# Routed experts of a decoder layer on one core: 17 tiles of 256 slots and 6 of 128 in place of 23 of 256

## The chip, the core and the metric

The kernel runs on one core of a Trainium2 chip. The metric is the device time in microseconds, the median of some runs. A core has TensorE (matmuls; PE in the profile, and PEld for its weight loads), VectorE (DVE), ScalarE (ACT), GpSimd (POOL) and SyncE (SP), which issues most transfers. Each engine works through its own instructions in order, and they wait for each other on semaphores.

## The reference

One decoder layer on x of shape (4, 512, 512): a gated linear recurrence, cross attention over 1601 context rows, and a block of causal self attention and a mixture of experts. Each is added to x, and a layer norm follows. The change lies in the experts:

```python
h = _rms(x, w_ln2).reshape(B * S, H)            # 2048 rows of 512
probs = jax.nn.softmax(h @ w_router, axis=-1)   # 8 experts
top_w, top_i = jax.lax.top_k(probs, TOP_K)      # 2 for each row
g = jnp.einsum('th,ehi->eti', h, w_gate_e)      # inner width 352
u = jnp.einsum('th,ehi->eti', h, w_up_e)
y = jnp.einsum('eti,eih->eth', jax.nn.silu(g) * u, w_down_e)
routed = jnp.einsum('eth,te->th', y, combine)   # combine: top_w at top_i, else 0
sh = jax.nn.silu(h @ w_sh_gate) * (h @ w_sh_up) @ w_sh_down    # inner width 1408
sh = sh * jax.nn.sigmoid(h @ w_sh_eg)
x = x + (routed + sh).reshape(B, S, H)
```

## The kernel before

The last stage, `moe`, runs through a list of passes (`schedule`). Passes 0 to 11 are the shared expert on batches 0 and 1, in six units of its inner width. Then there are 23 routed tiles, one pass each. Then come 12 passes of the shared expert on batches 2 and 3. A pass computes gate and up products, chunk by chunk of the inner width (128, 128 and 96 for a routed tile), with the weights stationary and the rows of the tile moving. Every f32 product is done as three fp32r matmuls, hi x hi, lo x hi and hi x lo (`product3`), over four chunks of 128 inputs. So a routed chunk has 12 matmuls for gate and 12 for up, and a tile has 72, each with its own weights to load.

Each row of the input goes to two experts. So 4096 (row, expert) pairs are sorted by expert into slots. A tile of `TW` = 256 slots belongs to one expert. An expert's last tile is filled up with whatever lies in the slots. The count of rows of each expert is known on the chip only, so the number of tiles is the one that always suffices: 4088 // 256 + 8 = 23. Which expert's weights a tile takes is computed by VectorE in `places`: it counts tiles for each expert (`few`, `many`), sums them up (`upto_e`), moves each row's place behind the tiles of the experts before (`place`), and compares the running sums with each tile's number (`compared`, `expert`). GpSimd then scatters the rows into `slots` in DRAM (32 indirect transfers), and for each tile it picks the expert's weights by indirect transfers: `pick_up` twice (gate and up, 0.72 MB each, into the single buffer `up_raw`) and `pick_down` (0.79 MB, into `dn_raw`). A pick is issued when the weights before it in that buffer have been split into hi and lo.

Around a tile x, in TensorE's order: chunk 0 of x (24 matmuls); the down product of tile x - 1 (`down`: for each block of 128 rows 9 matmuls of 512 columns, with the activations stationary); gate of chunk 1; the transposes of the rows of tile x + 1 (`turn`: 8 of 128 x 128); up of chunk 1; chunk 2. `down` of a tile waits until VectorE has written the low part of its last activations (`low_act(2)`).

ScalarE's order in a pass: sigmoid(0), split_up of the next tile's gate weights, high_act(0), split_up of its up weights, the copies of the previous tile's y out of PSUM (one for each block of 128 rows), sigmoid(1), high_rows of the next tile (4), split_down, high_act(1), sigmoid(2), high_act(2). VectorE follows with gated(0), split_up, low_act(0), split_up, low_rows (4), gated(1), split_down, low_act(1), gated(2), low_act(2). gated is two multiplications: by the sigmoid, and by the up product. SyncE loads the rows of tile x + 2 after the transposes of x + 1, and stores y block by block. The slots of y are gathered and added to X during the second shared part (`combine`).

`places` runs on VectorE at the end of pass 0.

Of the kernel before, what the change touches and what calls it, by code (L numbers as in the profile page):

```python
# [16 lines left out]
ALU = mybir.AluOpType  # L17
ACT = mybir.ActivationFunctionType
AX_X = mybir.AxisListType.X

P = 128
# [1902 lines left out]
TW = 256  # L1924
NTILES = (B * T * 2 - NEXP) // TW + NEXP
SLOTS = NTILES * TW

# [31 lines left out]
def moe(nc, X, regions, ahead, hx, slots, ident, d, out):  # L1959
# [21 lines left out]
    with ExitStack() as stack:  # L1981
# [18 lines left out]
        before = m.sb("before", [P, NEXP, NEXP])  # L2000
        above = act_f.bitcast(BF16).rearrange("p (t i j) -> p t i j", t=NTILE, i=NEXP)
        equal_f = S.tile("m_equal", at_s, NTILE * NEXP * NEXP // 2)
        equal = equal_f.bitcast(BF16).rearrange("p (t i j) -> p t i j", t=NTILE, i=NEXP)
        compared = equal_f[:, 0:NTILES * NEXP].rearrange("p (j e) -> p j e", e=NEXP)
# [16 lines left out]
        many = m.sb("many", [P, NEXP])  # L2021
        upto_e = m.sb("upto_e", [P, NEXP])
        picked = m.sb("picked", [P, NTILE, NEXP])
        expert = m.sb("expert", [P, NTILES])
        slot = m.sb("slot", [P, 2, NTILE], mybir.dt.int32)
        up_row = m.sb("up_row", [P, 2, NTILES], mybir.dt.int32)
# [30 lines left out]
        def _(sp):  # L2057
# [26 lines left out]
            def store_rows(tile):  # L2084
                for s in range(TW // P):
                    n = tile * (TW // P) + s
                    sp.wait_ge(s_ye, n + 1)
                    sp.dma_start(yslots[n * P:(n + 1) * P], ys[:, n % NY]).then_inc(s_ys[n % NY], 16)
# [31 lines left out]
        def _(pool):  # L2120
# [5 lines left out]
            pool.iota(count_i[:], pattern=[[1, NTILES]], base=0, channel_multiplier=0).then_inc(s_const, 1)  # L2126
            pool.iota(part_i[:], pattern=[[0, 1]], base=0, channel_multiplier=1).then_inc(s_const, 1)
            pool.wait_ge(s_const, 7)
# [21 lines left out]
            def pick_up(tile):  # L2150
                for j in range(2):
                    pool.wait_ge(s_uplo[j], UNITS + tile)
                    pool.indirect_dma_start(up_raw[:, j].rearrange("p k n -> p (k n)"), None, d["up"],
                                            bass.IndirectOffsetOnAxis(up_row[:, j, tile:tile + 1], 0)).then_inc(s_up_picked[j], 16)

            def pick_down(tile):
                pool.wait_ge(s_dnlo, UNITS + tile)
                if tile == 0:
                    for i in range(RINGS):
                        pool.wait_ge(s_scat[i], 16 * 2 * len(range(i, NTILE, RINGS)))  # L2160
                pool.indirect_dma_start(dn_raw[:].rearrange("p i n -> p (i n)"), None, d["dn"],
                                        bass.IndirectOffsetOnAxis(dn_row[:, tile:tile + 1], 0)).then_inc(s_dn_picked, 16)
# [8 lines left out]
            for i in range(NY):  # L2171
                pool.wait_ge(s_ys[i], 16 * len(range(i, NTILES * TW // P, NY)))
# [13 lines left out]
        def _(act):  # L2186
# [18 lines left out]
            def high_rows(tile):  # L2205
                if tile >= 2:
                    act.wait_ge(s_gu, 2 * base(R0 + tile - 1))
                if tile == 0:
                    act.wait_ge(s_gu, 2 * base(R0 - 1))
                if tile == 1:  # L2210
                    act.wait_ge(s_gu, 2 * base(R0))
                for k in range(KC):
                    act.wait_ge(s_tt, 2 * tile + k // 2 + 1)
                    act.activation(t_hi[tile % 2][:, k, :], t_bank[k // 2][:, (k % 2) * TW:(k % 2 + 1) * TW], ACT.Copy,
                                   scale=w2[:, k:k + 1]).then_inc(s_thi, 1)
# [7 lines left out]
            for x in passes:  # L2223
                p, w = x.p, x.stage
                width = T if x.shared else TW
# [49 lines left out]
        def _(dve):  # L2275
# [11 lines left out]
            def gated(x, i):  # L2287
                n, rows, width = base(x.p) + i, x.chunks[i][1], T if x.shared else TW
# [9 lines left out]
            def low_act(x, i):  # L2298
                n, rows, width = base(x.p) + i, x.chunks[i][1], T if x.shared else TW
# [18 lines left out]
            dve.wait_ge(s_const, 10)  # L2318
# [13 lines left out]
            own.done(dve.tensor_copy(part_f[:], part_i[:]))  # L2332

# [6 lines left out]
            few = equal_f[:, 0:NEXP * NEXP].rearrange("p (e k) -> p e k", e=NEXP)  # L2340
            start = count_f[:, 0:NEXP].unsqueeze(1).to_broadcast([P, NEXP, NEXP])
            own.done(dve.scalar_tensor_tensor(few, start, float(TW), total.unsqueeze(2).to_broadcast([P, NEXP, NEXP]), ALU.mult, ALU.is_lt))
# [10 lines left out]
            def places():  # L2353
                own.done(dve.tensor_reduce(many[:], few, AX_X, ALU.add))
                own.wait()
                own.done(dve.tensor_tensor_scan(upto_e[:], ones[:, 0:NEXP], many[:], 0.0, ALU.mult, ALU.add))
                own.wait()
                own.done(dve.tensor_tensor(many[:], upto_e[:], many[:], ALU.subtract))
                own.wait()
                own.done(dve.scalar_tensor_tensor(by_expert(place[:]), many[:].unsqueeze(2).to_broadcast([P, NEXP, NTILE]), float(TW), by_expert(place[:]), ALU.mult, ALU.add))  # L2360
                own.done(dve.tensor_tensor(compared, upto_e[:].unsqueeze(1).to_broadcast([P, NTILES, NEXP]),
                                           count_f[:].unsqueeze(2).to_broadcast([P, NTILES, NEXP]), ALU.is_le))
# [34 lines left out]
            def low_rows(tile):  # L2397
                for k in range(KC):
                    dve.wait_ge(s_thi, KC * tile + k // 2 * 2 + 2)
                    dve.scalar_tensor_tensor(t_lo[tile % 2][:, k, :], t_bank[k // 2][:, (k % 2) * TW:(k % 2 + 1) * TW], w2[:, k:k + 1],  # L2400
                                             t_hi[tile % 2][:, k, :], ALU.mult, ALU.subtract).then_inc(s_tlo, 1)
# [71 lines left out]
        def _(pe):  # L2473
            def turn(tile):
# [5 lines left out]
                for k in range(KC):  # L2480
                    for s in range(TW // P):
# [26 lines left out]
            for x in passes:  # L2508
                p, w = x.p, x.stage
                if x.shared:  # L2510
                    hi, lo, width = h_hi[x.group], h_lo[x.group], T
                else:
                    hi, lo, width = t_hi[x.tile % 2], t_lo[x.tile % 2], TW
# [4 lines left out]
                for i, (r0, rows) in enumerate(x.chunks):  # L2518
# [3 lines left out]
                    for j in range(2):  # L2522
                        if n == 0:
                            pe.wait_ge(s_uplo[j], 1)
                        if i == 1 and j == 1 and p + 1 < NP and not passes[p + 1].shared:
                            turn(passes[p + 1].tile)
                        product3(pe, gu_bank[n % 2][j][0:rows, 0:width],
                                 lambda c: up_hi[:, w % 2, j, c, r0:r0 + rows], lambda c: up_lo[:, w % 2, j, c, r0:r0 + rows],
                                 lambda c: hi[:, c, :], lambda c: lo[:, c, :], KC).then_inc(s_gu, 1)
                    if i == 0 and p:  # L2530
                        down(passes[p - 1])
                    if i == 1:
                        if p == 0:
                            pe.wait_ge(s_mask, 1)
                            pe.wait_ge(s_const, 10)
# [99 lines left out]
```

## Time and profile before

| | |
|---|---|
| median of 3 runs | 2493.06 us (2492.18 to 2497.55) |
| profiled execution, its own time | 2495.78 us |
| its span, first to last instruction | 2494.1 us |
| TensorE busy | 2374.0 us, 95% |
| weight loads | 1537.8 us, 62% |
| VectorE, ScalarE, GpSimd busy | 1353.1, 1351.2, 927.6 us |
| mean granted TensorE clock | 0.99 of full speed |

The span and the time of one execution differ by what lies before the first and after the last instruction. Matmul records overlap, since a matmul is recorded until its last result is out. So the rate of TensorE is read from the distances between starts and not from the mean durations. Weight loads overlap each other in the same way.

### The profile page before, as it was taken

Reading aid. Unit: us, or ns where it says so; the run is one execution under the profiler, and the core shown is the slowest. Engines: PE = TensorE matmul, PEld = TensorE weight load, DVE = VectorE, ACT = ScalarE, POOL = GpSimd, SP = SyncE. Lnnn points to the kernel's source line nnn. Section 1 sums busy time; section 2 is a strip of 40 time slices with the busy share of each in tenths; the row PEclk is TensorE's granted clock in tenths of the full one; section 3 lists DMA queues with packets and bytes.
Section 4 is the critical chain, followed back from the end, with each engine's and each line's share of the span. In section 5 each row is a group of like instructions: output and inputs, shape, how many; then the busy total and the mean of one; then the engine's idle time right before and its main releaser. Section 6 shows DMA issues by size and latency. Waiting matters only on the chain. (4 is left out here: it accounts for less than half of the span.)

```text
span 2494.1 us, 39149 instructions
## 1 busy us (share of the span) xinstructions
PE 2374.0 (95%) x15376; PEld 1537.8 (62%) x15376; DVE 1353.1 (54%) x2105; ACT 1351.2 (54%) x1714; POOL 927.6 (37%) x610
## 2 busy tenths in 40 slices
PE   8999899999999999999998899998899999999997
PEld 6877444444444444444334556565588899999885
DVE  6676534434443434443413755555565677776785
ACT  4332577677766777667995443433422366665221
POOL 1237654565465535654212433332033021221320
PEclk9999899999999999999999999999899999999999
DMA  6003774667455764756745000001144277775430
GB/s 219 17 18 106 221 197 117 157 167 194 118 146 158 196 170 97 186 155 167 191 87 203 18 1 18 1 18 54 60 163 160 92 238 243 243 237 185 144 119 34
DMA packets 206935, 331.46 MB, mean 133 GB/s; under 512 B 71264, under 2 KB 125792, under 8 KB 206560
## 3 DMA queue, kind: packets, MB, share of 16 engines
q1 hardware_dynamic: 188256, 252.80, 35.8%
q0 software_dynamic: 16336, 72.23, 8.8%
q10 hardware_dynamic: 2160, 3.93, 0.5%
q8 instruction: 122, 2.00, 0.3%
q14 instruction: 61, 0.50, 0.1%
HBM read 241.53 MB, written 99.42 MB: 137 GB/s over the span
## 5 line engine op out<-in xcount | busy, mean ns | idle before, releaser
L1052 ACT ACTIVATE A_c_prob<-c_psum 128x1024 f32<-128x1024 f32 x832 | 786.8, 1029 | 277.4 <-PE c_psum L1302 271.3
L982 POOL TENSOR_TENSOR E_c_roots<-E_c_roots,c_half 128x32 f32<-128x32 f32 (+1 forms) x70 | 363.3, 5191 | 406.6 <-DVE E_c_roots L1069 406.5
L1311 PE MATMUL c_psum<-A_c_prob,c_vq 128*17 128x512 f32 x3328 | 415.4, 599 | 8.6 <-DVE c_oT L1204 8.3
L137 PE MATMUL c_psum<-E_c_w,E_c_c 128*128 128x512 f32 x1248 | 313.8, 401 | 3.1 <-DVEq L1189 2.2
L1302 PE MATMUL c_psum<-c_qq,c_kq 64*128 64x512 f32 x1664 | 287.9, 438 | 18.8 <-ACT A_c_prob L1052 11.3
L137 PEld LDWEIGHTS c_psum<-E_c_w,E_c_c 128*128 128x128 f32 x1248 | 227.4, 188 | 124.6 <-issue 41.0
L1302 PEld LDWEIGHTS c_psum<-c_qq,c_kq 64*128 64x128 f32 x1664 | 136.6, 185 | 167.2 <-ACT A_c_prob L1052 91.4
L1108 DVE COPY E_c_unit<-c_psum 128x256 f32<-128x256 f32 x89 | 37.8, 425 | 327.8 <-PE c_psum L137 327.8
L2504 PE MATMUL m_psum<-A_m_dn_hi,A_m_a 128*128 128x512 f32 (+1 forms) x628 | 204.3, 394 | 2.2 <-DVE A_m_a L2301 2.2
L137 PE MATMUL m_psum<-R_m_t,m_up_hi 128*128 128x256 f32 (+1 forms) x1104 | 200.0, 283 | 0.0
L1311 PEld LDWEIGHTS c_psum<-A_c_prob,c_vq 128*17 128x17 f32 x3328 | 68.6, 96 | 188.4 <-issue 163.7
L1742 DVE TENSOR_REDUCE s_topx<-s_psum 128x4 f32<-128x2048 f32 (+1 forms) x64 | 95.5, 1492 | 146.2 <-PE s_psum L1860 137.0
L137 PEld LDWEIGHTS m_psum<-R_m_t,m_up_hi 128*128 128x128 f32 (+1 forms) x1104 | 165.8, 179 | 2.1
L2240 ACT ACTIVATE A_m_a<-Q_m_work 128x256 fp32r<-128x256 f32 (+2 forms) x113 | 56.7, 502 | 200.9 <-DVE Q_m_work L2296 159.2
L137 PE MATMUL m_psum<-R_m_t,m_up_lo 128*128 128x256 f32 (+1 forms) x552 | 154.7, 280 | 0.0
L1653 ACT ACTIVATE A_s_pT<-s_psum 128x2048 f32<-128x2048 f32 (+1 forms) x64 | 79.5, 1242 | 121.2 <-PE s_psum L1874 120.9
L2504 PEld LDWEIGHTS m_psum<-A_m_dn_hi,A_m_a 128*128 128x128 f32 (+1 forms) x628 | 117.8, 188 | 28.6 <-DVE A_m_a L2301 2.7
L137 PE MATMUL r_psum<-E_x,E_w_hi 128*128 128x512 f32 x384 | 121.0, 397 | 10.0 <-DVE E_w_lo L414 9.2
L2233 ACT ACTIVATE Q_m_work<-m_psum 128x256 f32<-128x256 f32 (+2 forms) x113 | 51.9, 459 | 134.2 <-PE m_psum L137 134.2
L2504 PE MATMUL m_psum<-Q_m_dn_lo,A_m_a 128*128 128x512 f32 (+1 forms) x314 | 123.1, 392 | 0.0
L975 POOL TENSOR_TENSOR E_c_c<-E_c_raw,E_c_c 128x512 fp32r<-128x512 f32 x89 | 118.7, 1333 | 7.1
L137 PE MATMUL m_psum<-R_g_hi,m_up_hi 128*128 128x512 f32 x264 | 105.6, 400 | 3.6 <-DVE m_up_lo L2278 3.6
(316 smaller groups left out, 4216.7 us busy)
## 6 DMA issues: line engine op xcount, KB each, us to landing
c_kq<-kd SPq DMA_DIRECT2D x248, 208.0 KB, 6.1
kd<-S_c_t SPq DMA_DIRECT2D x96, 256.0 KB, 4.0
E_c_raw<-in_ctxT SPq DMA_DIRECT2D x89, 256.0 KB, 4.2
qd<-A_c_q SPq DMA_DIRECT2D x64, 256.0 KB
c_qq<-qd SPq DMA_DIRECT2D x64, 256.0 KB, 3.1
vd<-A_c_vt SPq DMA_DIRECT2D x104, 136.0 KB, 3.0
c_vq<-vd SPq DMA_DIRECT2D x31, 442.0 KB, 9.0
R_m_hs<-slots SPq DMA_DIRECT2D x23, 512.0 KB
```

What stands on the lines that cost most here:

```text
L137: mm = pe.matmul(out, a(c), b(c), start=first and i == 0, stop=last and i == len(terms) - 1)
L975: pool.tensor_tensor(c_lo[:, job % 2], c_raw[:, n % CB], c_hi[:, job % 2], ALU.subtract).then_inc(s_clo, 1)
L982: pool.tensor_tensor(rr[:, unit % RB, 0:n], ms[:, unit % RB, 0:n], half[:, 0:n], ALU.pow).then_inc(s_r, 1)
L1052: act.activation(prob[:, t % PB, 2 * (u % 2):2 * (u % 2) + 2, :], score_banks[u % 3], ACT.Exp, scale=XD ** -0.5).then_inc(s_ex, 1)
L1108: dve.tensor_copy(raw[:, unit % RB, at:at + HD], src[:, 0:HD]).then_inc(s_k, 1)
L1302: mm = pe.matmul(score_banks[u % 3][:, s, :], kq[rows, q % 2, u % 2, kt * P:(kt + 1) * P], qq[rows, q % 2, u % 2, :], start=True, stop=True)
L1311: mm = pe.matmul(o_bank[32 * j:32 * j + VW, :], vq[:, q % 2, kt, j, :], prob[:, t % PB, j, :], start=kt == 0, stop=kt == CT - 1)
L1653: act.activation(pT[:, kt % 2, :, 0:L], psum[:, 0:HPC, 0:L], ACT.Exp, scale=SCALE).then_inc(s_ex, 1)
L1742: dve.reduce_max(topx[:, t, ::SD], psum[:, 0:HPC, 0:(t + 1) * P], AX_X).then_inc(s_top, 1)
L2233: act.activation(sig[0:rows, 0:width], gu_bank[n % 2][0][0:rows, 0:width], ACT.Sigmoid).then_inc(s_sig, 1)
L2240: act.activation(a_hi[0:rows, p % 2, i, 0:width], act_f[0:rows, 0:width], ACT.Copy).then_inc(s_ahi, 1)
L2504: mm = pe.matmul(y_bank[t], a[0:rows, p % 2, i, ts], w[0:rows, i, :], start=k == 0, stop=k == 3 * len(x.chunks) - 1)
```

## The change

There are still 23 tiles, but 17 of them are pairs of halves (256 slots) and 6 are single halves (128 slots), 40 halves in all against 46. An expert with n rows gets full pairs for its rows; if the number of its halves is odd, the last half goes to a single, and when the singles are used up, to a pair of its own where room is. The tiles are worked on in the order pair, pair, pair, single, five times over, and then pair, pair, single. All widths of a routed pass follow `x.width`, 256 or 128. `places` computes the new positions and the experts of the tiles.

```diff
-NTILES = (B * T * 2 - NEXP) // TW + NEXP
-SLOTS = NTILES * TW
+PAIRS, SINGLES = 17, 6
+HALVES = 2 * PAIRS + SINGLES
+NTILES = PAIRS + SINGLES
+SLOTS = HALVES * P
+def order_of_tiles():
+    out, pair = [], 0
+    for single in range(SINGLES):
+        upto = min(3 * single + 3, PAIRS)
+        out += [*range(pair, upto), PAIRS + single]
+        pair = upto
+    return out
+ORDER = order_of_tiles()
+first_half = lambda column: 2 * column if column < PAIRS else column + PAIRS
...
-        self.subs = TT if self.shared else TW // P
+        self.subs = TT if self.shared else 1 + (ORDER[tile] < PAIRS)
+        self.width = self.subs * P
...
-                rows = slots[tile * TW:(tile + 1) * TW].rearrange("(s p) n -> p s n", p=P)
-                sp.dma_start(hs[:, tile % 2], rows).then_inc(s_hs[tile % 2], 16)
+                at, subs = first_half(ORDER[tile]), passes[R0 + tile].subs
+                rows = slots[at * P:(at + subs) * P].rearrange("(s p) n -> p s n", p=P)
+                sp.dma_start(hs[:, tile % 2, 0:subs], rows).then_inc(s_hs[tile % 2], 16)
...
-            pool.iota(count_i[:], pattern=[[1, NTILES]], base=0, channel_multiplier=0).then_inc(s_const, 1)
+            pool.iota(count_i[:, 0:PAIRS], pattern=[[2, PAIRS]], base=0, channel_multiplier=0).then_inc(s_const, 1)
+            pool.iota(count_i[:, PAIRS:NTILES], pattern=[[1, SINGLES]], base=2 * PAIRS, channel_multiplier=0).then_inc(s_const, 1)
+            pool.iota(ranks_i, pattern=[[1, 2 * NEXP]], base=0, channel_multiplier=0).then_inc(s_const, 1)
...
-                                            bass.IndirectOffsetOnAxis(up_row[:, j, tile:tile + 1], 0)).then_inc(s_up_picked[j], 16)
+                                            bass.IndirectOffsetOnAxis(up_row[:, j, ORDER[tile]:ORDER[tile] + 1], 0)).then_inc(s_up_picked[j], 16)
...
             def places():
-                own.done(dve.tensor_reduce(many[:], few, AX_X, ALU.add))
+                own.done(dve.tensor_scalar(below, ranks_f[:, 0:NEXP], -float(NEXP), None, ALU.add))
+                own.done(dve.tensor_reduce(np_e, few[:, :, 1::2], AX_X, ALU.add))
+                own.done(dve.tensor_reduce(ns_e, few[:, :, 0::2], AX_X, ALU.add))
...
+                own.done(dve.scalar_tensor_tensor(turn_e, singles_e, pairs, ns_e, ALU.add, ALU.subtract))
+                own.wait()
+                own.done(dve.tensor_scalar(single_at, turn_e, float(PAIRS), pairs, ALU.min, ALU.max))
+                own.wait()
+                own.done(dve.tensor_tensor(single_at, single_at, turn_e, ALU.add))
...
-                    for s in range(TW // P):
+                    for s in range(passes[R0 + tile].subs):
...
-                        product3(pe, gu_bank[n % 2][j][0:rows, 0:width],
+                        product3(pe, gu_bank[n % 2][j][0:rows, 0:x.width],
                                  lambda c: up_hi[:, w % 2, j, c, r0:r0 + rows], lambda c: up_lo[:, w % 2, j, c, r0:r0 + rows],
-                                 lambda c: hi[:, c, :], lambda c: lo[:, c, :], KC).then_inc(s_gu, 1)
+                                 lambda c: hi[:, c, 0:x.width], lambda c: lo[:, c, 0:x.width], KC).then_inc(s_gu, 1)
```

In `places`, 20 VectorE instructions stand in place of 5; the part shown as "..." goes on in the manner of the lines around it. `high_rows`, `low_rows`, `gated`, `low_act`, `sigmoid` and `high_act` take `width` where they had 256.

## Rows read from the trace of the kernel before

**Rows 1.** The page, busy time of the engines.
```profile
PE 2374.0 (95%) x15376; PEld 1537.8 (62%) x15376; DVE 1353.1 (54%) x2105; ACT 1351.2 (54%) x1714; POOL 927.6 (37%) x610
```

**Rows 2.** Chain that ended last, in order of time: start, us, what.
```profile
1795.32 13.95 PE m_psum L137 x48
...
1831.62 5.48 PE m_psum L2504 x24
...
2095.31 0.88 PE m_psum L2482 x8
2096.18 7.10 PE m_psum L137 x60
2103.29 4.25 PE m_psum L2504 x18
2107.54 1.43 PE m_psum L137 x12
```

**Rows 3.** Timeline, the transposes in a routed pass: start, us, engine, line, operation.
```profile
2108.70 0.90 PEld L2482 LDWEIGHTS m_psum<-ident,R_m_hs 128*128 128x128 f32 x8
```

**Rows 4.** Timeline of TensorE in the first stage.
```profile
54.61 0.95 PE L551 MATMUL r_psum<-r_ones,r_sumsq 128*128 128x1 f32 x8
...
55.42 0.48 PE L137 MATMUL r_psum<-E_w_hi,E_o 128*128 128x512 f32 x1
```

**Rows 5.** Timeline of TensorE, attention scores with 128 moving columns.
```profile
1495.51 0.40 PE L1868 MATMUL s_psum<-Q_s_qk,Q_s_qk 32*128 32x128 f32 x8
...
1495.73 0.28 PE L1872 MATMUL s_psum<-s_negm,s_sel 32*128 32x128 f32 x4
```

**Rows 6.** Groups by line and shape, weight loads: busy us, mean ns.
```profile
L137 PEld LDWEIGHTS m_psum<-R_m_t,m_up_hi 128*128 128x128 f32 x736 | 114.6, 188 | 2.1
L137 PEld LDWEIGHTS m_psum<-R_m_t,m_up_hi 128*96 128x96 f32 x368 | 51.2, 162 | 0.0
```

**Rows 7.** Timelines of TensorE, ScalarE, VectorE and GpSimd in one routed pass.
```profile
2123.23 0.48 PE L137 MATMUL m_psum<-R_m_t,m_up_hi 128*128 128x256 f32 x2
...
2130.42 0.46 PE L2504 MATMUL m_psum<-A_m_dn_hi,A_m_a 128*128 128x512 f32 x1
...
2124.58 1.50 ACT L2203 ACTIVATE A_m_dn_hi<-Q_m_dn_raw 128x1536 fp32r<-128x1536 f32 x1
...
2131.66 1.37 ACT L2194 ACTIVATE m_up_hi<-S_up_raw 128x1408 fp32r<-128x1408 f32 x1
...
2124.01 1.66 DVE L2400 SCALAR_TENSOR_TENSOR R_m_t<-m_psum,S_w,R_m_t 128x256 fp32r<-128x256 f32 x4 [2.65 <-ACT R_m_t L2214]
...
2129.91 0.42 DVE L2301 TENSOR_TENSOR A_m_a<-Q_m_work,A_m_a 96x256 fp32r<-96x256 f32 x1 [0.48 <-ACT A_m_a L2240]
...
2121.63 0.94 POOL L2153 DMA_INDIRECT S_up_raw<-in_up,m_up_row  x1 [0.99 <-DVE m_up_lo L2278]
```

**Rows 8.** Two stretches: busy us of each engine, granted clock, DMA share, GB/s.
```profile
2128.30:2129.10 0.80, 0.80 (x9) 0.80 (x8) 0.68 (x3) 0.00 (x0) 0.70 (x1) 1.00 0.09 37
2133.10:2133.90 0.80, 0.80 (x5) 0.67 (x4) 0.80 (x2) 0.41 (x1) 0.55 (x1) 1.00 0.00 0
```

**Rows 9.** Timeline of VectorE in passes 0 and 1.
```profile
1809.88 0.29 DVE L2338 TENSOR_TENSOR S_m_place<-S_m_place,m_psum 128x128 f32<-128x128 f32 x1
...
1814.59 0.21 DVE L2354 TENSOR_REDUCE m_many<-S_m_equal 128x8 f32<-128x64 f32 x1
...
1815.45 0.34 DVE L2361 TENSOR_TENSOR S_m_equal<-m_upto_e,m_count_f 128x184 f32<-128x184 f32 x1
...
1818.96 0.69 DVE L2293 TENSOR_TENSOR Q_m_work<-m_psum,Q_m_work 128x512 f32<-128x512 f32 x1
...
1827.55 0.69 DVE L2301 TENSOR_TENSOR A_m_a<-Q_m_work,A_m_a 128x512 fp32r<-128x512 f32 x1 [0.70 <-ACT A_m_a L2240]
```

**Rows 10.** What touches the slots: count, ns least/median/most, first and last start.
```profile
L2082 SPq DMA_DIRECT2D R_m_hs<-slots x23: 360/439/649, 1959.0 to 2258.7; - x23
...
L2147 POOL DMA_INDIRECT slots<-A_m_spare,m_slot x16: 959/972/1922, 1825.6 to 1914.3; - x16
```

More of the change, by code:

```diff
@@ L2020, in moe @@
         rank = S.tile("m_rank", at_s + NEXP * NTILE, NTILE, NEXP)
-        many = m.sb("many", [P, NEXP])
-        upto_e = m.sb("upto_e", [P, NEXP])
+        np_e, ns_e, pairs_e, singles_e, pair_at, turn_e, single_at, shift, below = (restart[:, i * NEXP:(i + 1) * NEXP] for i in range(9))
         picked = m.sb("picked", [P, NTILE, NEXP])
@@ L2211, in high_rows @@
                     act.wait_ge(s_gu, 2 * base(R0))
+                width = passes[R0 + tile].width
                 for k in range(KC):
                     act.wait_ge(s_tt, 2 * tile + k // 2 + 1)
-                    act.activation(t_hi[tile % 2][:, k, :], t_bank[k // 2][:, (k % 2) * TW:(k % 2 + 1) * TW], ACT.Copy,
+                    act.activation(t_hi[tile % 2][:, k, 0:width], t_bank[k // 2][:, (k % 2) * TW:(k % 2) * TW + width], ACT.Copy,
                                    scale=w2[:, k:k + 1]).then_inc(s_thi, 1)
@@ L2224, in _ @@
                 p, w = x.p, x.stage
-                width = T if x.shared else TW
+                width = x.width
                 prev = passes[p - 1] if p else None
@@ L2287, in gated @@
             def gated(x, i):
-                n, rows, width = base(x.p) + i, x.chunks[i][1], T if x.shared else TW
+                n, rows, width = base(x.p) + i, x.chunks[i][1], x.width
                 dve.wait_ge(s_sig, n + 1)
@@ L2298, in low_act @@
             def low_act(x, i):
-                n, rows, width = base(x.p) + i, x.chunks[i][1], T if x.shared else TW
+                n, rows, width = base(x.p) + i, x.chunks[i][1], x.width
                 dve.wait_ge(s_ahi, n + 1)
@@ L2332, in _ @@
             own.done(dve.tensor_copy(part_f[:], part_i[:]))
+            own.done(dve.tensor_copy(ranks_f[:], ranks_i))
             by_expert = lambda ap: ap.rearrange("p (e t) -> p e t", e=NEXP)
@@ L2339, in _ @@
             total = by_expert(upto[:])[:, :, NTILE - 1]
-            few = equal_f[:, 0:NEXP * NEXP].rearrange("p (e k) -> p e k", e=NEXP)
-            start = count_f[:, 0:NEXP].unsqueeze(1).to_broadcast([P, NEXP, NEXP])
-            own.done(dve.scalar_tensor_tensor(few, start, float(TW), total.unsqueeze(2).to_broadcast([P, NEXP, NEXP]), ALU.mult, ALU.is_lt))
+            few = few_f.rearrange("p (e k) -> p e k", e=NEXP)
+            start = ranks_f[:].unsqueeze(1).to_broadcast([P, NEXP, 2 * NEXP])
+            own.done(dve.scalar_tensor_tensor(few, start, float(P), total.unsqueeze(2).to_broadcast([P, NEXP, 2 * NEXP]), ALU.mult, ALU.is_lt))
             own.wait()
@@ new lines, in places @@
+                own.done(dve.scalar_tensor_tensor(turn_e, singles_e, pairs, ns_e, ALU.add, ALU.subtract))
[3 more added lines that the diff above has]
+                own.done(dve.tensor_tensor(single_at, single_at, turn_e, ALU.add))
+                own.wait()
+                own.done(dve.scalar_tensor_tensor(shift, pairs_e, -2.0, single_at, ALU.mult, ALU.add))
+                own.done(dve.scalar_tensor_tensor(by_expert(behind), each(np_e), float(TW), placed, ALU.mult, ALU.is_le))
@@ new lines, in places @@
+                own.done(dve.tensor_tensor(ns_e, ns_e, below, ALU.mult))
+                own.wait()
+                own.done(dve.tensor_tensor(by_expert(behind), by_expert(behind), each(shift), ALU.mult))
+                own.done(dve.scalar_tensor_tensor(placed, each(pair_at), float(TW), placed, ALU.mult, ALU.add))
+                own.done(dve.scalar_tensor_tensor(compared, per_tile(pairs_e), 2.0, halves, ALU.mult, ALU.is_le))
+                own.done(dve.tensor_tensor(matched, per_tile(single_at), halves, ALU.is_equal))
@@ L2363, in places @@
+                own.wait()
+                own.done(dve.scalar_tensor_tensor(place[:], behind, float(P), place[:], ALU.mult, ALU.add))
+                own.done(dve.tensor_tensor(matched, matched, per_tile(ns_e), ALU.mult))
+                own.wait()
+                own.done(dve.tensor_tensor(compared, compared, matched, ALU.add))
                 own.wait()
@@ L2480, in turn @@
                 for k in range(KC):
-                    for s in range(TW // P):
+                    for s in range(passes[R0 + tile].subs):
                         tr = pe.transpose(t_bank[k // 2][:, (k % 2) * TW + s * P:(k % 2) * TW + (s + 1) * P],
@@ L2510, in _ @@
                 if x.shared:
-                    hi, lo, width = h_hi[x.group], h_lo[x.group], T
+                    hi, lo = h_hi[x.group], h_lo[x.group]
                 else:
-                    hi, lo, width = t_hi[x.tile % 2], t_lo[x.tile % 2], TW
+                    hi, lo = t_hi[x.tile % 2], t_lo[x.tile % 2]
                     pe.wait_ge(s_tlo, KC * (x.tile + 1))
```

39 lines of the change are left out of this document (24 added, 15 removed).

## The prediction

> **What bounds the kernel now.** The page comes first: TensorE is busy for 95% of the span, VectorE and ScalarE for 54% each [rows 1], and the mean granted clock is 0.99, its upper level nearly throughout. The chain that ended last is to be read next. From 1795 us on, through the expert stage up to the last pass, it consists of TensorE alone [rows 2]. A routed tile repeats four pieces: 8 transposes in 0.87 us, 60 product matmuls in 7.10, 18 down matmuls in 4.25, 12 product matmuls in 1.43. Their sum is 13.65 us, and 23 tiles have this period. So whatever shortens TensorE's stream in a tile counts in full, until another engine or a transfer becomes late. The rates in that stream: 7.10/60 = 118.3 ns a product matmul of 256 columns, 4.25/18 = 0.236 us a down matmul of 512 columns, 0.87/8 = 0.109 us a transpose.
>
> **The change, step by step.** The number of tiles stays 23, so the weight picks (46 and 23 indirect transfers), the weight splits and the 72 product matmuls a tile stay. Six tiles have 128 slots instead of 256. In such a tile:
> - One block of 128 rows instead of two goes through the down product: 9 matmuls fewer, 9 x 0.236 = 2.12 us.
> - 4 transposes fewer: 4 x 0.109 = 0.44 us.
> - 72 product matmuls stream 128 columns instead of 256. Each still loads its own weights, and here is the choice on which the sum hangs. If only columns counted, a matmul would fall to about 60 ns: from 512 to 256 columns it falls by 118 ns, 0.46 a column, and 118.3 - 128 x 0.46 = 59. But three places show a floor above that. Transposes with 128x128 weights and 128 moving columns start every (0.90 - 0.14)/7 = 0.109 us [rows 3]. In the first stage, eight matmul records with 128x128 weights and a single moving column begin at 54.61 and the next matmul at 55.42: 0.81/8 = 0.101 us, though there is hardly anything to stream [rows 4]. And in the attention scores, whose operands are fp32r tiles as here and whose moving side has 128 columns, eight matmuls (two sets of four that run side by side, 32 rows each) take from 1495.51 to the next set at 1495.73, 0.11 us a set [rows 5]. All of this fits one load of 128 weight columns. The load records agree: 188 ns for 128 columns, 162 for 96 [rows 6], that is 0.81 ns a column on a fixed part, so about 104 ns of loading proper for 128 columns. I take 0.109 us for the 48 matmuls of the two 128-row chunks. They save 48 x 0.0093 = 0.45 us.
> - The third chunk has 96 weight columns. No row shows it with few moving columns. From the records it loads 26 ns faster, 0.083 us, and 24 matmuls save 24 x 0.035 = 0.85 us. The other bound is 0.108 us, if what rows 5 show is the moving side at half rate and not the load: then 24 x 0.010 = 0.24 us. I take 0.083, because with one moving column the floor is nearly as high [rows 4], which a moving side can't cause.
>
> Sum for a small tile: 2.12 + 0.44 + 0.45 + 0.85 = 3.86 us; six give 23.2 us (19.5 with the other value for the 96 columns).
>
> The Trainium skill (TensorE: Matmul & The Clock Gate, section LDWEIGHTS) puts a load at columns/1.2 ns, which is 107 and 80 ns, and says that row count does not matter. By its figures the sum would be 48 x 0.012 + 24 x 0.038 + 2.56 = 4.05 us a tile, 24 in all; it speaks for the 0.083, and for carrying rows 5, with 32 rows, over to 128.
>
> **What could become late.** The saving is spread over three passes, since a pass holds the down product of the tile before it and the transposes of the one behind it. The pass before a small tile takes 13.65 - 0.44 = 13.2 us, its own 13.65 - 1.30 = 12.35, the one after it 13.65 - 2.12 = 11.5. No pass falls to the 9.8 that a small tile alone would make.
>
> The nearest wait today is that of the down product for the low part of the last chunk (low_act): VectorE starts it at 2129.91 and needs 0.42, and the down product starts at 2130.42, so 0.1 us is left [rows 7]. Walk the same chain behind a small tile. The transposes in its pass end at T (2123.23 in the rows' pass; the down product starts at T + 7.2 there). ScalarE's high_rows and split_down keep their size, and VectorE's split_down can start where ScalarE's ends, at T + 2.9 (2126.08). It takes 1.7 to the next start, low_act(1) 0.36, gated(2) 0.6, ScalarE 0.33, low_act(2) 0.3: T + 6.2. The short ones are scaled to what 128 x 128 elements cost in rows, 0.29 us [rows 9]. TensorE arrives at T + 12 x 0.109 + 24 x 0.083 + 24 x 0.118 and the 0.1 which the rows' pass has on top: T + 6.2. So this is even, and costs 0 to 0.1 us a tile. Ahead of a small tile its first chunk takes 2.6 us instead of 2.84, but its narrow high_rows and low_rows release the engines 0.4 us earlier: 0.35 us left.
>
> Behind a small tile VectorE also loses 2.12 us between its last split_up and low_rows (2124.01), where it now idles for 2.65 [rows 7]: 0.5 us stays.
>
> The picks: both up transfers are issued by 2122.6, and the engines' DMA share is near 1 until 2128.3, then 0.09 for 0.8 us [rows 7, 8]; ScalarE takes up the second half at 2131.66. In a pass of 11.5 us it would do so at 2129.5, 1.2 us after the landing. The down pick, issued behind VectorE's split_down, has landed when the share is 0 (2133.10) and is taken up at 2124.58 + 13.65 = 2138.2, or 2136.1 then. Both are covered. If they were not, each us of lateness would hold ScalarE's queue (the copies of y, sigmoid(1), high_rows) and through them TensorE.
>
> **Routing arithmetic.** `places` gets 20 VectorE instructions for 5. 12 small ones at about 0.2 us, 4 on 128 elements at 0.29, 4 on 184 at 0.34: about 4.9 us, for 1.20 removed (1814.59 to 1815.79) [rows 9]. The 3.7 us delay gated(2) from 1818.96 to 1822.7; its chunk's bank is wanted at 1826.05. low_act of the next chunk ends at 1828.24 now; with idle time of VectorE taken up it would end at 1831.0, wanted at 1831.62 [rows 2, 9]. Covered by some 0.6 us; without cover it would cost up to 3.7 us once. The slots come 3.9 us later, and so do the 32 scatters (the last at 1914.3), while the first load of rows is at 1959.0 [rows 10]: 40 us of cover. Three more iotas and casts of 0.15 us lie in idle time. SP loads and stores less (half of 6 tiles), and waits nowhere new.
>
> **The sum** is made against the profiled execution, 2495.78 us (span 2494.1 and 1.7 around it): 2495.8 - 23.2 = 2472.6, and with 0.3 us for the even wait 2472.9. It ran 2.7 us over the median of the runs, so the forecast for the median is 2470.2, call it 2470.
>
> **Rivals.**
> - A: narrow matmuls run below the load floor. For it: weight loads overlap each other here already (records of 188 ns every 118). Against it: rows 3 to 5. At 60 ns a small tile would save 72 x 0.058 + 2.56 = 6.7 us, but VectorE's chain holds two downs back: the tile's own first chunk lasts 1.4 us against a chain end at 2.3, 0.9 us, and behind the tile 36 x 0.06 + 2.84 + 0.1 = 5.1 stands against 6.2, 1.1 us. So 4.7 us a tile, 28 in all: 2465. The same page of the Trainium skill (section Back-to-back issue gap) has about 81 ns for a sustained pair of load and matmul at 128 columns; by it a tile would save 72 x 0.037 + 2.56 = 5.2 less some 0.9 of waiting, 26 in all, 2467. The trace has no such row for fp32r. 10%.
> - B: the weights arrive too late. Three weight transfers must pass a tile whatever its width. For it: each pick waits for a split, and its buffer is the only one. Against it: some 2.4 us of every 13.65 have a share under 0.1 (three slices of 0.8, two of them among the rows) [rows 8], so 11.2 us would do, and the shortest pass is 11.5. If it held half of the saving back: 2481; all of it: 2493. 11%.
> - C, on the other side: an fp32r matmul with few moving columns is done in two passes, each with its load, as the plain f32 matmuls of rows 4 are (four calls, eight records). Then 0.216 us a matmul, 72 x 0.098 = +7.0 - 2.56 = +4.5 us a tile: 2520. It decides from 0.154 us a matmul on (2.56/72 above 118.3). Against it: rows 5, where fp32r with 128 columns keeps 0.108 us, though with 32 rows only. 5%.
> - D: the 96-column chunk does not gain (moving side at half rate): 2474. It lies inside the forecast's own range.
>
> **Chances and range.** The forecast with D: 74%, its own range 2467 to 2476. A 10%, B 11% (a quarter of it within 0.2% of no change), C and the like 5%. 0.2%, 5 us, is about what a measurement of this kernel tells from no change. Faster 0.92, same 0.03, slower 0.05. To leave no more than two in ten outside, the range goes from 2462, A's less the 2 to 3 us that its waits are uncertain by, to 2479, where B holds back 9 us.
>
> **What would show it.** In the profile after: the product matmuls of the six tiles 0.109 us apart, 0.083 in the third chunk; passes of 13.2, 12.35 and 11.5 us; 9 down matmuls in 2.1 us; no wait of TensorE on VectorE above 0.1 us; the DMA share near 1 for longer. The forecast is wrong if small tiles show other spacings, if ScalarE waits for a pick, or if the chain of waits leaves TensorE.

## The result and the profile after

| | before | after |
|---|---|---|
| median of 4 runs each, side by side | 2495.31 us (2492.18 to 2499.41) | 2474.99 us (2472.85 to 2476.81) |
| profiled execution, its span | 2495.78, 2494.1 us | 2476.71, 2475.0 us |

The ratio is 0.9919, with a 95% interval of 0.9905 to 0.9933: 20.3 us faster. The forecast was 2470.0, in a range of 2462 to 2479. It had taken 23.1 us off a median of 2493.06; with a fourth run the median of before is 2495.31.

The page of the kernel after, busy time (TensorE does 78 matmuls less: 6 x 9 down, 6 x 4 transposes) [rows 1]:

```profile
PE 2357.1 (95%) x15298; PEld 1522.0 (61%) x15298; DVE 1346.1 (54%) x2121; ACT 1341.0 (54%) x1708; POOL 932.0 (38%) x612
```

The chain that ended last, after: start, us, what. It answers to [rows 2]. First a full tile and a small one with its neighbour, then the end of the routed stage:

```profile
2112.05 4.25 PE m_psum L2555 x18
2116.31 1.43 PE m_psum L137 x12
2117.73 0.44 PE m_psum L2533 x4
2118.17 6.91 PE m_psum L137 x60
2125.07 4.22 PE m_psum L2555 x18
2129.29 1.29 PE m_psum L137 x12
2130.59 0.90 PE m_psum L2533 x8
2131.48 6.23 PE m_psum L137 x60
2137.71 2.13 PE m_psum L2555 x9
2139.84 1.43 PE m_psum L137 x12
...
2149.24 4.21 PE m_psum L2555 x18
...
2268.07 10.29 PE m_psum L137 x72
2278.35 2.06 PE m_psum L2555 x9
2280.41 11.14 PE m_psum L137 x48
```

How to read it: the piece of 60 matmuls that begins at 2118.17 holds 36 with 256 columns and the small tile's first 24 with 128. So 24 narrow ones take 6.91 - 36 x 0.1183 = 2.65 us, 0.110 each. The next 12 take 1.29, 0.108 each. The piece at 2131.48 holds 12 more of these (1.30), the 24 of the 96-column chunk, and 24 wide ones (2.84): 6.23 - 1.30 - 2.84 = 2.09 us, 0.087 each. The timeline shows the same directly, every third matmul 0.25 to 0.26 us after the one before:

```profile
2132.61 0.33 PE L137 MATMUL m_psum<-R_m_t,m_up_hi 128*96 128x128 f32 x2
2132.78 0.25 PE L137 MATMUL m_psum<-R_m_t,m_up_lo 128*96 128x128 f32 x1
2132.86 0.33 PE L137 MATMUL m_psum<-R_m_t,m_up_hi 128*96 128x128 f32 x2
```

Per small tile that is 2.12 (4.25 - 2.13, down) + 0.44 (transposes) + 0.19 + 0.14 + 0.87 (the pieces of products: 7.10 - 6.91, 1.43 - 1.29, 7.10 - 6.23) = 3.76 us, six give 22.6. The distances between down products say the same: 13.02, 12.64 and 11.53 us around the small tile instead of three times 13.65, 3.76 in all. Counted as the forecast counts passes, from first product to first product, the same pieces make 13.21, 12.45 and 11.53 (13.65 less 0.44, 1.20 and 2.12), where 13.2, 12.35 and 11.5 were forecast.

Where the time went, for the whole span. From the first routed transposes to the end of the last routed down product, before took 1972.80 to 2300.23, 327.4 us; after took 1975.41 to 2280.41, 305.0 us: 22.4 less. From there to the end of the last down product both take 166.2, from the first product of the stage to the first routed transposes both 177.5. The span is 19.1 shorter. The missing 3.3 us lie outside: 0.7 behind the last down product, and 2.6 ahead of the stage, which begins at 1795.51 instead of 1792.93, in code that the change does not touch. There the granted clock differs. Stretches of after: length, busy us of TensorE, its weight loads, VectorE, ScalarE and GpSimd with their counts, granted clock, DMA share, GB/s:

```profile
1410.00:1420.00 10.00, 8.44 (x82) 4.81 (x80) 5.07 (x7) 3.17 (x3) 3.82 (x3) 0.88 0.00 0
1420.00:1430.00 10.00, 9.31 (x85) 6.29 (x78) 4.74 (x3) 2.95 (x3) 3.62 (x4) 0.60 0.01 2
1740.00:1750.00 10.00, 8.41 (x77) 5.90 (x79) 6.03 (x6) 3.09 (x4) 0.00 (x0) 0.83 0.01 2
```

The same stretches of before are granted 1.00, the whole of the self attention between 1350 and 1760 too. Its score matmuls start over 404.4 us in before (1353.5 to 1757.9) and over 408.2 in after (1352.4 to 1760.6).

### The profile page after: what moved, and what is told of

Its sections match the earlier page's. It is cut to its first block and busy times, and to the rows that moved or that the text cites. A ratio compares the mean times of both kernels' runs of the same rounds, so it can differ in the third digit from the quotient of the medians.

```text
span 2475.0 us, 38993 instructions
## 1 busy us (share of the span) xinstructions
PE 2357.1 (95%) x15298; PEld 1522.0 (61%) x15298; DVE 1346.1 (54%) x2121; ACT 1341.0 (54%) x1708; POOL 932.0 (38%) x612
## 5 line engine op out<-in xcount | busy, mean ns | idle before, releaser
L1302 PE MATMUL c_psum<-c_qq,c_kq 64*128 64x512 f32 x1664 | 288.3, 438 | 19.1 <-ACT A_c_prob L1052 11.2
L2555 PE MATMUL m_psum<-A_m_dn_hi,A_m_a 128*128 128x512 f32 (+1 forms) x592 | 193.9, 396 | 2.2 <-DVE A_m_a L2324 2.2
L137 PE MATMUL m_psum<-R_m_t,m_up_hi 128*128 128x256 f32 (+3 forms) x1104 | 192.8, 278 | 0.0
L2263 ACT ACTIVATE A_m_a<-Q_m_work 128x512 fp32r<-128x512 f32 (+4 forms) x113 | 54.7, 484 | 200.9 <-DVE Q_m_work L2319 199.6
L137 PE MATMUL m_psum<-R_m_t,m_up_lo 128*128 128x256 f32 (+3 forms) x552 | 152.8, 277 | 0.0
L2555 PEld LDWEIGHTS m_psum<-A_m_dn_hi,A_m_a 128*128 128x128 f32 (+1 forms) x592 | 112.0, 189 | 27.4 <-DVE A_m_a L2324 2.9
L2256 ACT ACTIVATE Q_m_work<-m_psum 128x512 f32<-128x512 f32 (+4 forms) x113 | 49.9, 442 | 128.4 <-PE m_psum L137 128.4
L2555 PE MATMUL m_psum<-Q_m_dn_lo,A_m_a 128*128 128x512 f32 (+1 forms) x296 | 116.8, 395 | 0.0
```

Of the source, the lines that this page charges most:

```text
L137: mm = pe.matmul(out, a(c), b(c), start=first and i == 0, stop=last and i == len(terms) - 1)
L1302: mm = pe.matmul(score_banks[u % 3][:, s, :], kq[rows, q % 2, u % 2, kt * P:(kt + 1) * P], qq[rows, q % 2, u % 2, :], start=True, stop=True)
L2256: act.activation(sig[0:rows, 0:width], gu_bank[n % 2][0][0:rows, 0:width], ACT.Sigmoid).then_inc(s_sig, 1)
L2263: act.activation(a_hi[0:rows, p % 2, i, 0:width], act_f[0:rows, 0:width], ACT.Copy).then_inc(s_ahi, 1)
L2555: mm = pe.matmul(y_bank[t], a[0:rows, p % 2, i, ts], w[0:rows, i, :], start=k == 0, stop=k == 3 * len(x.chunks) - 1)
```

## The experiments

Every kernel below is the kernel after with the edit shown. "Routed stage" is the stretch just defined, 327.4 us before and 305.0 after; it does not contain the self attention. The time given is one run beside seven or nine of the kernel before, or a median where an interval stands.

### wide_products: the narrow products streamed wide

```diff
-                        product3(pe, gu_bank[n % 2][j][0:rows, 0:x.width],
+                        product3(pe, gu_bank[n % 2][j][0:rows, 0:T if x.shared else TW],
...
-                                 lambda c: hi[:, c, 0:x.width], lambda c: lo[:, c, 0:x.width], KC).then_inc(s_gu, 1)
+                                 lambda c: hi[:, c, 0:T if x.shared else TW], lambda c: lo[:, c, 0:T if x.shared else TW], KC).then_inc(s_gu, 1)
```

> The changed kernel, but the product matmuls of the six small tiles stream 256 columns again (the upper 128 are results that nobody reads); the down product, transposes, copies and transfers stay small. The routed stage, from the first transposes of routed rows to the end of the last routed tile's down product, took 327.4 us before and 305.0 after. Theory (three separate terms that add up): only 6 x (2.12 + 0.44) = 15.4 us are left of the gain, so 312.1 us. Rival (part of the narrow matmuls' gain is eaten by waits and comes back when they are wide): less than 311.

Measured: 2479.60 us; routed stage 1972.64 to 2283.95, 311.3 us. The expectation had 312.1, or less than 311 for its rival, and the run lies between: 0.8 us below the sum of the separate terms, 0.3 above the bound of the rival. The last routed pieces of its chain:

```profile
2270.65 11.25 PE m_psum L137 x72
2281.90 2.05 PE m_psum L2555 x9
```

Narrowing the products is worth 6.3 us in six tiles, 1.05 a tile, and the rest, 16.1 us or 2.69 a tile, comes from the matmuls that a tile no longer has. The product pieces alone show more (7.13, 1.42 and 7.11 here around the small tile, 6.91, 1.29 and 6.23 in after: 1.23), but the down pieces next to them are shorter here (4.13 and 2.08 against 4.22 and 2.13), which takes 0.14 back. Why they are shorter stays open; it moves the border between the two shares by 0.15 us a tile and leaves their sum.

### cols64: 64 moving columns

The products of a small tile stream 64 columns; the activations of the other half of its rows are made from what lies in PSUM, so what is stored for them is not the reference's.

```diff
-                        product3(pe, gu_bank[n % 2][j][0:rows, 0:x.width],
+                        product3(pe, gu_bank[n % 2][j][0:rows, 0:64 if x.width == P else x.width],
...
-                                 lambda c: hi[:, c, 0:x.width], lambda c: lo[:, c, 0:x.width], KC).then_inc(s_gu, 1)
+                                 lambda c: hi[:, c, 0:64 if x.width == P else x.width], lambda c: lo[:, c, 0:64 if x.width == P else x.width], KC).then_inc(s_gu, 1)
```

> The changed kernel, but the product matmuls of the six small tiles stream only 64 columns: half of a small tile's rows are left out. Theory (a narrow product matmul is bound by the load of its own 128 or 96 weight columns): the spacings stay 0.108 and 0.087 us and the routed stage stays at 305 us, within 0.5. Rival (the moving side runs at half rate when narrow, 0.108 us for 128 columns): the matmuls fall to about half, 3.7 us less a tile, some of it lost again to VectorE's chain; the stage ends at 290 to 297 us.

Measured: 2477.57 us; routed stage 308.0 us. The chain around the same small tile:

```profile
2115.93 6.88 PE m_psum L137 x60
2122.81 4.25 PE m_psum L2555 x18
2127.06 1.26 PE m_psum L137 x12
2128.32 0.92 PE m_psum L2533 x8
2129.25 7.77 PE m_psum L137 x60
2137.01 2.07 PE m_psum L2555 x9
```

Half the moving columns save next to nothing: 6.88 for 6.91, 1.26 for 1.29. So the 0.108 us (128 weight columns) and 0.087 (96) go by the weight columns, and what a matmul streams is hidden. That this is the time of its load is argued from that and from the load records (188 and 162 ns); no run here streams through one load twice. Rival A, which has narrow matmuls run below this floor, is out.

The stage is 3.0 us longer than in after, where 0.5 at most had been expected. It sits in two places, 7.77 instead of 6.23 here and 11.83 instead of 10.29 behind the last small tile. In both the clock fell, in stretches of this kernel that are at 1.00 in after:

```profile
2130.00:2140.00 10.00, 10.00 (x72) 9.63 (x72) 7.97 (x16) 6.46 (x11) 1.59 (x2) 0.83 0.74 273
2270.00:2280.00 10.00, 10.00 (x53) 8.40 (x53) 4.48 (x9) 2.32 (x6) 0.00 (x0) 0.83 0.36 107
```

The timeline shows where, behind the last small tile: the narrow matmuls end with their usual spacing, and the wide ones behind them come 0.43 us apart, and then 0.30 and 0.23 again.

```profile
2271.84 0.48 PE L137 MATMUL m_psum<-R_g_hi,m_up_hi 128*128 128x512 f32 x1
...
2272.51 0.63 PE L137 MATMUL m_psum<-R_g_hi,m_up_lo 128*128 128x512 f32 x1
2272.94 0.63 PE L137 MATMUL m_psum<-R_g_hi,m_up_hi 128*128 128x512 f32 x1
...
2275.07 0.63 PE L137 MATMUL m_psum<-R_g_hi,m_up_lo 128*128 128x512 f32 x1
2275.50 0.46 PE L137 MATMUL m_psum<-R_g_hi,m_up_hi 128*128 128x512 f32 x1
```

0.43 us for 512 columns is the lower of the clock's two levels (1.2 GHz), 0.23 the upper (2.4). It cost 1.54 us at each place, at two of six small tiles, in the one execution of this kernel.

### small_last: six small tiles in a row

```diff
 def order_of_tiles():
-    out, pair = [], 0
-    for single in range(SINGLES):
-        upto = min(3 * single + 3, PAIRS)
-        out += [*range(pair, upto), PAIRS + single]
-        pair = upto
-    return out
+    return list(range(NTILES))
```

> The changed kernel, with the six small tiles one after the other behind the 17 large ones. TensorE's own work is the same, but small passes in a row are 9.9 us long, where the weights' three transfers have to keep up (2.75 MB, 278 GB/s). Theory (transfers are covered: issue to landing of the second up pick shrinks with the rows and the y that are smaller too, to about 5.3 us, and a wait of 0 to 0.2 us a tile on VectorE): 305 to 306 us for the routed stage. Rival (the weights' transfers need 11.2 us a tile): 6 x 1.3 us more, 312 to 314.

Measured: 2476.99 us; routed stage 306.2 us, where 305 to 306 had been expected and 312 to 314 by the rival. (The 2.75 MB of the expectation are the three weight transfers, 2.23, and a small tile's rows and y.) The 4 transposes of the later small tiles begin at 2218.87, 2228.77, 2239.04, 2249.03 and 2259.68: passes of 9.90, 10.27, 9.99 and 10.65 us, against 9.89 for a small tile alone (13.65 - 3.76). First ScalarE's waits for weight transfers from 1990 us on (us in total, times, longest), then two timelines, TensorE's two waits and VectorE ahead of the first of them:

```profile
ACT m_up_hi L2211 <- DMA S_up_raw<-in_up,m_up_row: 2.7, 3, 1.5
```

```profile
2235.55 0.51 PE L2550 MATMUL m_psum<-A_m_dn_hi,A_m_a 128*128 128x512 f32 x1 [0.15 <-DVE A_m_a L2319]
2256.21 0.50 PE L2550 MATMUL m_psum<-A_m_dn_hi,A_m_a 128*128 128x512 f32 x1 [0.27 <-DVE A_m_a L2319]
```

```profile
2234.23 0.29 DVE L2311 TENSOR_TENSOR Q_m_work<-m_psum,Q_m_work 96x128 f32<-96x128 f32 x1 [0.44 <-issue]
```

So even where every pass carries its three transfers, the stage is only 1.2 us longer than in after, and not all of that is theirs. The first wait of TensorE, in the pass of 10.27, comes before ScalarE's first wait for a transfer (one of 0.86 us that ends at 2237.67). Ahead of it VectorE stood still for 0.44 us in front of `gated(2)`, and the profile names no cause. The second, in the pass of 10.65, comes behind ScalarE's longest wait, 1.53 us until 2248.33; this pass is 0.76 us over. Rival B's mechanism exists, but it costs less than 1 us here, and its price begins only below the passes of 11.5 us that the change makes; in after ScalarE waits for no pick.

### p16s7, p16s7_again and after_again: one pair less, one single more

```diff
-PAIRS, SINGLES = 17, 6
+PAIRS, SINGLES = 16, 7
...
-        upto = min(3 * single + 3, PAIRS)
+        upto = (single + 1) * PAIRS // SINGLES
```

> 16 pairs and 7 singles, 39 halves, still 23 tiles, spread evenly. Theory (a tile that is small instead of large is worth 3.76 us wherever it stands): the routed stage 301.2 us, the kernel 3.8 us faster than the changed one. Rival (denser small tiles begin to wait, here two large ones between them at times): 303 us or more.

> The changed kernel unchanged, timed again beside the kernel before and beside p16s7_again. Theory (the routed stage gives 22.4 us and nothing else in the kernel moves; what differs from that in a run is TensorE's clock in code that the change leaves alone): 22 to 23 us faster than before in the median, within 2 of it. Rival (something outside the routed stage costs 2 to 3 us in the changed kernel): 19 to 20 us again.

> 16 pairs and 7 singles again. Theory: 3.5 us faster than after_again (the routed stage took 301.5 us against 305.0). Rival (no seventh gain over the whole kernel): same as after_again within 1 us.

Measured:

| kernel | median us | kernel before beside it | ratio, 95% | routed stage |
|---|---|---|---|---|
| p16s7 | 2469.84 (2468.98 to 2476.92) | 2498.43 | 0.9890, 0.9874 to 0.9907 | 301.6 |
| after_again (kernel after, no edit) | 2474.37 (2471.31 to 2477.72) | 2495.59 | 0.9910, 0.9895 to 0.9924 | 305.1 |
| p16s7_again | 2468.83 (2466.68 to 2472.71) | 2495.59 | 0.9895, 0.9880 to 0.9910 | 301.7 |

The routed stage of p16s7 had been expected at 301.2; its trace is of its slowest run, 2476.92 us, the other three took 2468.98 to 2470.12.

A seventh single costs nothing in room: the most halves that 4096 pairs of row and expert over 8 experts need is 4088 // 128 + 8 = 39, which is 2 x 16 + 7, and 17 and 6 make 40. `places` gives the last half of an expert a free pair first and a single when no pair is free, and it lays a pair beyond the last column of pairs on two singles, so every split of the rows has room.

after_again is 21.2 us faster than the kernel before beside it, between the 22 to 23 expected and the 19 to 20 of the rival, and the interval (19 to 26 us) decides nothing; its routed stage of 305.1 us says that the stage repeats. Side by side the seventh single gains 5.5 us in the medians, more than the 3.5 expected, and the runs of the two overlap (2471.31 to 2477.72, 2466.68 to 2472.71). The traces give 3.4 in the routed stage and 3.6 from the stage's first product to the end of the last routed down product: after_again takes 1796.14 to 2278.77, 482.6 us, and p16s7_again 1791.31 to 2270.37, 479.1. What the medians show beyond that is not the seventh single's: in these two profiled executions the stage starts 4.8 us apart, behind code that is the same. The chain of p16s7_again shows the same pieces for its last small tile as that of after:

```profile
2246.91 6.91 PE m_psum L137 x60
...
2258.03 10.29 PE m_psum L137 x72
2268.32 2.06 PE m_psum L2555 x9
```

### p22s1: one single alone

```diff
-PAIRS, SINGLES = 17, 6
+PAIRS, SINGLES = 22, 1
...
-        upto = min(3 * single + 3, PAIRS)
+        upto = PAIRS
```

> 22 pairs and one single at the end: the new routing arithmetic with hardly any of its use. Theory (a small tile gives 3.7 us wherever it stands, the longer arithmetic of places lies wholly under TensorE's work): routed stage 323.7 us, and from the stage's first product matmul to the first routed transposes 177.5 us as before. Rival (the arithmetic shows): this stretch 178.5 us or more.

Measured: 2492.67 us, one run; routed stage 323.9 us, 3.5 less than before, and the stretch from the first product (1795.51) to the first routed transposes (matmul at 1972.92) 177.4, as in before (1795.32, 1972.64: 177.3). So one single gives one sixth of the saving less 0.2 to 0.3 us, a wait of TensorE on VectorE at 2239.99 that has nothing to do with the single, and the new routing arithmetic, all of which this kernel has, costs TensorE 0.1 us at most.

### places_long: 3.9 us more on VectorE

Ahead of the copy into `slot`, at the end of `places`:

```diff
+                for _ in range(12):
+                    own.done(dve.tensor_tensor(picked[:], rank[:], rank[:], ALU.add))
+                    own.wait()
```

> The changed kernel with 12 more VectorE instructions on 128 x 128 elements at the end of places, each waiting for the one before, 3.8 us in all, whose result is not used. In the changed kernel low_act of the second chunk of pass 1 ends at 1832.7 and TensorE comes to wait for it at 1834.2, so 1.5 us are left. Theory (that is the cover): the down product of pass 1 starts 2.3 us late, the stretch from the first product matmul to the first routed transposes is 179.8 us instead of 177.5, and the routed stage stays 305. Rival (the cover is larger, since VectorE catches up in idle time): 177.5.

Measured: 2478.22 us, one run. TensorE's waits from 1795 to 1980 (the first is there in every kernel, before the stage's first product):

```profile
PE m_psum L137 <- DVE m_up_lo L2301: 3.7, 1, 3.7
PE m_psum L137 <- DVE Q_m_work L2319: 1.4, 1, 1.4
PE m_psum L2558 <- DVE A_m_a L2324: 0.8, 1, 0.8
```

The same moments in its timelines, TensorE's two and VectorE's two:

```profile
1828.43 0.48 PE L137 MATMUL m_psum<-R_g_hi,m_up_hi 128*128 128x512 f32 x1 [1.38 <-DVE Q_m_work L2319]
1835.08 0.50 PE L2558 MATMUL m_psum<-A_m_dn_hi,A_m_a 128*128 128x512 f32 x1 [0.81 <-DVE A_m_a L2324]
```

```profile
1822.75 3.88 DVE L2431 TENSOR_TENSOR m_picked<-S_m_rank 128x128 f32<-128x128 f32 x12
...
1834.33 0.69 DVE L2324 TENSOR_TENSOR A_m_a<-Q_m_work,A_m_a 128x512 fp32r<-128x512 f32 x1 [0.70 <-ACT A_m_a L2263]
```

The stretch from the first product to the first routed transposes is 1796.31 to 1976.37, 180.1 us, against 177.3 in after (179.8 against 177.5 had been expected): of 3.9 us on VectorE 2.75 come through. TensorE first waits for the bank that `gated(2)` empties (1.4), then the down product waits for `low_act` of the next chunk (0.8). The down product starts 38.77 us behind the first product, 36.13 in after, 2.64 late, where 2.3 was expected of it. So the cover that after has left is 1.2 to 1.3 us (3.9 less 2.75 or 2.64). The routed stage is 305.4 us, 0.4 longer: VectorE's stop of 0.44 us in front of `gated(2)` is there once in this kernel too, and the down product behind it starts late, at 1998.09.

## Why the prediction was right, point by point

**The sum of a small tile.** 3.86 us was forecast, 3.76 measured:

| term | forecast | measured |
|---|---|---|
| 9 down matmuls | 2.12 | 2.12 |
| 4 transposes | 0.44 | 0.44 |
| 48 products, 128 weight columns | 0.45 | 0.46 (0.19 + 0.14 + 0.13; 0.110 and 0.108 us each) |
| 24 products, 96 weight columns | 0.85 | 0.74 (0.87 - 0.13; 0.087 us each) |

The mis-sized term is the last: 0.087 us a matmul instead of 0.083, 0.1 us a tile. Cut the other way, by wide_products, the products give 1.05 and the vanished matmuls 2.69; the sum is the same. The choice on which the sum hung, that the weight load is the floor at 128 moving columns [rows 3 to 5], held: cols64 shows that the moving columns are not the floor, and the 96-column chunk that the weight columns are. The load of 96 columns is a shorter one, as the load records of 188 and 162 ns said [rows 6], by 0.021 us for the 0.026 read off them; the other bound, 0.108, is refuted, and rival D with it. The Trainium skill (TensorE: Matmul & The Clock Gate, section LDWEIGHTS) gives by its rule of columns over 1.2 ns an estimate of 107 and 80 ns for these loads; the first agrees with the 0.108 us measured, the second is 0.007 us under the 0.087.

**The narrow matmuls below the floor (A).** Not so: 0.108 to 0.110 with 128 columns, and 0.105 with 64 (1.26 / 12). The same page of the Trainium skill (section Back-to-back issue gap) has about 81 ns for a pair of load and matmul at 128 columns; here, with fp32r operands, it is 108, and the forecast that followed from the 81 ns, 2467, did not come.

**Two passes with a load each (C).** Not so: 0.108 us, where it needed 0.216, with 128 rows as with the 32 of [rows 5].

**The chain behind a small tile.** It was forecast as even. Timelines of VectorE and TensorE, after:

```profile
2137.15 0.29 DVE L2324 TENSOR_TENSOR A_m_a<-Q_m_work,A_m_a 96x128 fp32r<-96x128 f32 x1 [0.38 <-ACT A_m_a L2263]
...
2142.67 1.66 DVE L2451 SCALAR_TENSOR_TENSOR R_m_t<-m_psum,S_w,R_m_t 128x256 fp32r<-128x256 f32 x4 [0.44 <-ACT R_m_t L2237]
```

```profile
2137.55 0.45 PE L2555 MATMUL m_psum<-A_m_dn_hi,A_m_a 128*128 128x512 f32 x1
```

`low_act(2)` ends at 2137.44, the down product starts at 2137.55: 0.1 us left, T + 6.3 with T = 2131.24, where T + 6.2 was forecast. It has no wait beside it, and TensorE waits for nobody in the whole routed stage. So the 0.3 us that the sum had set aside for it were not spent. VectorE's idle time ahead of `low_rows` is 0.44, forecast 0.5.

That 0.1 us is all the cover, and that after never waits is partly luck. In all nine traces of the new code VectorE stands still once in the routed stage, for 0.44 us in front of `gated(2)`, and the profile names no cause. In after it does so in the pass ahead of a small tile, where there is more cover:

```profile
2224.68 0.42 DVE L2316 TENSOR_TENSOR Q_m_work<-m_psum,Q_m_work 96x256 f32<-96x256 f32 x1 [0.44 <-issue]
```

In small_last, p22s1, places_long and both p16s7 kernels it falls elsewhere, and the down product behind it starts 0.3 us late. The prediction has no term for such a stop. It also accounts for most of what the seventh single misses of 3.76 us.

**The picks (B).** Covered, as forecast, at passes down to 11.5 us. GpSimd issues them as before but for the first up pick in the pass of each small tile that still has picks: it is recorded with 2.28 us instead of 0.94 [rows 7], in all five of them, and the second goes out 0.66 us later for it. Why stays open; it held up nothing:

```profile
2127.46 2.28 POOL L2175 DMA_INDIRECT S_up_raw<-in_up,m_up_row  x1 [3.90 <-DVE m_up_lo L2301]
```

small_last ran passes of 9.9 to 10.65 us. So the 11.2 us that the prediction put as the least that the transfers allow was wrong: it took the time that the engines stood busy in a pass of 13.65 us for the time that they need.

**Routing arithmetic.** The instructions between the end of `low_act(0)` of pass 1 and the first `picked` take 1817.20 to 1821.44, 4.24 us, against 1.24 before: 3.0 us more, forecast 3.7. The small instructions overlap, so that together they take less than their records. VectorE in after:

```profile
1821.44 0.38 DVE L2415 SCALAR_TENSOR_TENSOR m_picked<-S_m_rank,S_m_place 128x128 f32<-128x128 f32 x1
...
1824.57 0.69 DVE L2316 TENSOR_TENSOR Q_m_work<-m_psum,Q_m_work 128x512 f32<-128x512 f32 x1
...
1832.03 0.69 DVE L2324 TENSOR_TENSOR A_m_a<-Q_m_work,A_m_a 128x512 fp32r<-128x512 f32 x1 [0.70 <-ACT A_m_a L2263]
```

The last one ends at 1832.72 and its reader starts at 1834.07 in the timeline: 1.35 us left where 0.6 had been forecast, and places_long confirms it with 1.3 (its 3.9 us made the down product 2.64 late). The difference is the shorter arithmetic, 0.7 us.

**The total, and the step that was mis-sized.** In the routed stage 22.4 us were gained of 22.9 forecast (23.2 less 0.3). The median came out 5.0 us above the forecast. 0.5 of it is the stage. 2.7 are the step "it ran 2.7 us over the median of the runs, so the forecast for the median is 2470.2": it took the median of three runs as the kernel's own. The kernel before had medians of 2495.31, 2498.43 and 2495.59 in three sets of 4 to 9 runs, so that its profiled execution of 2495.78 was an ordinary one, and 2472.9 was the number to forecast. The last 1.8 us go with the granted clock. The four runs of after are 2472.85 and 2473.26 us with a mean clock of 0.990 and 0.991, and 2476.71 and 2476.81 with 0.988; the execution of before that the sum starts from had 0.990. Every other run of the two kernels whose clock is on record sorts in the same way (those of after are counted in):

| mean granted clock | before, 16 runs | after and after_again, 9 runs |
|---|---|---|
| 0.990 and 0.991 | 2492.83 to 2496.21, median 2495.0 | 2471.31 to 2474.37, median 2472.9 |
| below 0.990 | 2497.19 to 2500.35, median 2498.6 | 2475.07 to 2477.72, median 2476.8 |

Like against like the change gains 22.2 and 21.9 us, which is what the routed stage shows, and the 20.3 of the medians is this less the luck of which runs fell where. After's trace shows one source of such a difference, 2.6 us ahead of the stage beside three stretches of self attention with a granted clock of 0.60 to 0.88. What sets the clock off there stays open: the code is the same in all kernels, and small_last, places_long and p16s7 ran with it, wide_products, p22s1 and after_again without.

## What to carry to other kernels

When tiles are made smaller, count first the instructions that vanish and then the floor of those that stay: here 16.1 of 22.4 us came from matmuls that no longer exist, and halving the columns of the rest gave only 6.3, because a floor that goes by the weight columns, and that the trace of before shows elsewhere (transposes, one-column matmuls, the load records), ends the gain. Compare two versions by the length of the stage that was changed: it is 305.0 and 305.1 us in two executions in which the stage starts at 1795.5 and 1793.7, and that alone is about half of what a small tile is worth. And if a sixth small tile pays 3.8 us, try the seventh: 16 pairs and 7 singles give 2468.8 us beside 2474.4, the best version here, 1.05% under the kernel before.

## What the runs showed of the hardware that was not expected

- Behind short matmuls that are back to back TensorE's granted clock can fall. In cols64, behind 72 matmuls of 64 moving columns that are bound by their weights, the 512-column matmuls started 0.43 us apart instead of 0.23 for some 3 us, 1.54 us of loss, and the same loss came at one more of its six small tiles. With 128 columns it was seen at no small tile of after, after_again, both p16s7 kernels, small_last, p22s1 and places_long. So fewer moving columns can make a stage longer, though the narrow matmuls themselves are not slower. It is one execution, and what the clock goes by isn't shown.
- A matmul of 64 moving columns is hardly faster than one of 128 (1.26 and 1.29 us for 12), if each loads 128 weight columns.
- VectorE stands still for 0.44 us without a recorded cause, once in the routed stage of each of the nine traces of the new code and not in that of before. Where the cover is 0.1 us, TensorE starts 0.3 us late for it.
